# VectorE forms products of whole groups, ScalarE sums them and takes one silu a group, and four rows of a tile change engines

## The reference

```
h = einsum('btc,pc->btp', silu(einsum('btd,cd->btc', x, W_up) + b_up), W_down) + b_down
... scores of two sets of 64 keys for 8 heads, top 8 of each, top 8 of their 64 sums -> sc, indices
de = down_embed[indices]                  # 64 rows of 256 for every token
ue = up_embed[indices]                    # 64 rows of 512 for every token
z = einsum('btd,bthkd->bthk', h, de)      # 64 dot products with h
z = silu(z * softmax(sc))
out = einsum('bthk,bthkd->btd', z, ue)    # weighted sum of 64 rows
x = layernorm(x + out)
```

## Time and profile before

| | us |
|---|---|
| runs: median (lowest to highest) of 3 | 3196.2 (3188.67 to 3196.66) |
| span of the profiled execution, first to last instruction | 3168.2 |
| runs above that span | 20.5 to 28.5 |
| TensorE busy | 2818.4 |
| VectorE busy | 2783.2 |
| ScalarE busy | 2105.8 |
| GpSimd busy | 2098.0 |

### The profile page before, as it was taken

The page is one execution under the profiler, slowest core; times in us unless marked ns, Lnnn a source line. Parts: engine busy times, 40 slices in busy tenths (PEclk is TensorE's granted clock), DMA queues, the critical chain, the costliest instruction groups (busy, mean ns, idle before and its releaser), DMA issues.

```text
span 3168.2 us, 39919 instructions
## 1 busy us (share of the span) xinstructions
PE 2818.4 (89%) x9216; PEld 1501.1 (47%) x9216; DVE 2783.2 (88%) x10160; ACT 2105.8 (66%) x6641; POOL 2098.0 (66%) x2056
## 2 busy tenths in 40 slices
PE   7998999999899999999999999899899999998963
PEld 4444455545454545444445444444445454444431
DVE  3488999999989899999999899898999999898987
ACT  4476766767776667776666677666676666677642
POOL 0067666677667677666667767667766666766676
PEclk9999999999999999999999999999999999999986
DMA  8078888888888788888888888888888888888888
GB/s 289 16 265 277 276 270 269 274 283 289 275 270 267 261 282 293 279 281 269 269 275 300 263 277 280 265 268 291 270 278 275 271 275 290 282 279 275 269 296 280
DMA packets 189837, 856.45 MB, mean 270 GB/s; under 512 B 36192, under 2 KB 39392, under 8 KB 189088
## 3 DMA queue, kind: packets, MB, share of 16 engines
q0 software_dynamic: 163840, 805.44, 76.5%
q1 hardware_dynamic: 19104, 34.87, 3.2%
q10 hardware_dynamic: 6656, 13.60, 1.2%
HBM read 845.38 MB, written 8.39 MB: 269 GB/s over the span
## 4 chain that ended last, share of the span: by engine, by line
PE 57%; POOL 11%; DVE 10%; DMA 10%; ACT 6%; issue 6%; SPq 0%; DVEq 0%; ACTq 0%; POOLq 0%
PE bank L465 14%; POOL ring L279 11%; DMA ring<-embed,idx 10%; PE bank L508 8%; PE bank L362 7%; PE bank L481 6%; PE bank L342 5%; DVE bank L1166 4%; PE bank L496 4%; PE bank L444 3%; PE bank L371 3%; ACT xc L691 3%; DVE ring L1152 2%; PE bank L472 2%; ACT raw L688 1%
## 5 line engine op out<-in xcount | busy, mean ns | idle before, releaser
L279 POOL DMA_INDIRECT ring<-embed,idx x2048 | 2096.7, 1024 | 1057.9 <-issue 544.3
L1166 DVE SCALAR_TENSOR_TENSOR bank<-ring,coef,bank 128x512 f32<-128x512 f32 x1312 | 990.8, 755 | 7.4 <-issue 0.2
L1152 DVE SCALAR_TENSOR_TENSOR ring<-ring,hcur 128x256 f32<-128x256 f32 x2048 | 827.1, 423 | 185.7 <-DMA ring<-embed,idx 182.6
L508 PE MATMUL bank<-ring,diag_c 128*128 128x512 f32 x1344 | 668.8, 628 | 119.6 <-ACT diag_c L666 103.9
L657 ACT ACTIVATE coef<-prob,zp 128x1 f32<-128x1 f32 x2048 | 459.1, 293 | 456.1 <-DVE ring L1152 454.9
L465 PE MATMUL bank<-w_up,zs 128*128 128x512 f32 x1024 | 490.4, 630 | 69.2 <-ACT zs L779 65.8
L508 PEld LDWEIGHTS bank<-ring,diag_c 128*128 128x128 f32 x1344 | 246.6, 199 | 385.8 <-issue 224.9
L465 PEld LDWEIGHTS bank<-w_up,zs 128*128 128x128 f32 x1024 | 200.7, 201 | 329.7 <-issue 238.6
L997 DVE SCALAR_TENSOR_TENSOR xc<-raw,taps,xc 128x128 f32<-128x128 f32 x960 | 266.0, 351 | 53.8 <-ACT xc L691 53.8
L342 PE MATMUL bank<-w_in,ut 128*128 128x512 f32 (+1 forms) x768 | 285.1, 524 | 4.4 <-ACT seg L679 4.3
L666 ACT ACTIVATE diag_c<-cst,coef 128x128 f32<-128x128 f32 x672 | 234.8, 394 | 49.4 <-PE bank L508 38.9
(11 more groups left out here) (147 smaller groups left out, 3685.1 us busy)
## 6 DMA issues: line engine op xcount, KB each, us to landing
ring<-embed,idx POOLq DMA_INDIRECT x2048, 4.6
ring<-uT SPq DMA_DIRECT2D x4, 2048.0 KB, 14.3
ut<-uT SPq DMA_DIRECT2D x32, 256.0 KB, 6.5
zs<-u SPq DMA_DIRECT2D x32, 256.0 KB, 5.7
out<-acc SPq DMA_DIRECT2D x32, 256.0 KB, 4.7
w_up<-W_upT ACTq DMA_DIRECT2D x1, 4096.0 KB, 12.7
w_in<-W_in ACTq DMA_DIRECT2D x1, 2560.0 KB, 17.0
w_in<-W_in ACTq DMA_DIRECT2D x1, 2048.0 KB, 21.5
```

The costliest lines, as they stand in the source:

```text
L279: pool.indirect_dma_start(out=ring[:, k % RING, :], out_offset=None, in_=embed, in_offset=bass.IndirectOffsetOnAxis(ap=idx[:, half, k:k + ...
L508: m = pe.matmul(bank[SUM][:, :], diag_c[:, (len(PE_ROWS) * t + n) % DIAGS, :], ring[:, k % RING, DP:ROW], start=(n == 0), stop=(n == len(P ...
L1152: m = dve.scalar_tensor_tensor(out=ring[:, k % RING, 0:DP], in0=ring[:, k % RING, 0:DP], scalar=1.0, in1=hcur[:, :], op0=ALU.mult, op1=ALU ...
L1166: dve.scalar_tensor_tensor(out=total if n == len(DVE_ROWS) - 1 else running[:, :], in0=ring[:, k % RING, DP:ROW], scalar=coef[:, k:k + 1], ...
```

## The change

Ten groups (3, 5, 7, 8, 9, 10, 11, 13, 16, 19; `SUMMED`), 35 picks of a tile, are handled in another way. VectorE waits for all rows of such a group, multiplies all their 256 numbers by h in one tensor_tensor (`products`), in place in `ring`, and goes on to the weighs of group g-2, which now stand behind the product without dots between them. ScalarE copies each row's products over themselves with the pick's `prob` as scale and sums them into `zp`, waits for its own last sum (`zp_ok`), and takes one silu over the whole group. Groups 1, 13, 16 and 19 turn one P into D: TensorE has 17 rows a tile instead of 21, VectorE weighs 47 instead of 43.

```diff
-GROUPS = ("DD", "PPPD", "DD", "DDD", "PPD", "DDD", "DD", "DDD", "PDDD", "DDD", "DDD", "DDDD", "PDD", "PPPD", "PP", "PDD", "PPPP", "D", "DDD", "PPPD", "D", "PDD")
+GROUPS = ("DD", "PPDD", "DD", "DDD", "PPD", "DDD", "DD", "DDD", "PDDD", "DDD", "DDD", "DDDD", "PDD", "PPDD", "PP", "PDD", "PPPD", "D", "DDD", "PPDD", "D", "PDD")
+SUMMED = (3, 5, 7, 8, 9, 10, 11, 13, 16, 19)
...
                 act.wait_ge(dot_ok, NGRP * t + g + 1)
-                for k in range(FIRST[g], FIRST[g + 1]):
-                    m = act.activation(coef[:, k:k + 1], prob_v[:, k:k + 1], ACT.Silu, scale=zp[:, k:k + 1])
+                if g in SUMMED:
+                    for k in range(FIRST[g], FIRST[g + 1]):
+                        m = act.activation(ring[:, k % RING, 0:DP], ring[:, k % RING, 0:DP], ACT.Copy,
+                                           scale=prob_v[:, k:k + 1], accum_out=zp[:, k:k + 1])
+                    m.then_inc(zp_ok, 1)
+                    act.wait_ge(zp_ok, len(SUMMED) * t + SUMMED.index(g) + 1)
+                    m = act.activation(coef[:, FIRST[g]:FIRST[g + 1]], zp[:, FIRST[g]:FIRST[g + 1]], ACT.Silu)
+                else:
+                    for k in range(FIRST[g], FIRST[g + 1]):
+                        m = act.activation(coef[:, k:k + 1], prob_v[:, k:k + 1], ACT.Silu, scale=zp[:, k:k + 1])
                 m.then_inc(coef_ok, 1)
...
+            def products(t, g):
+
+                lo, hi = FIRST[g], FIRST[g + 1]
+                for k in range(lo, hi):
+                    dve.wait_ge(row_in[k % RING], 16 * (uses(k) * t + k // RING + 1))
+                of = ring[:, lo % RING:lo % RING + hi - lo, 0:DP]
+                dve.tensor_tensor(of, of, hcur[:, :].unsqueeze(1).to_broadcast([P, hi - lo, DP]), ALU.mult).then_inc(dot_ok, 1)
...
+                if g in SUMMED:
+                    products(t, g)
                 for n in range(max(len(mine), len(late))):
-                    if n < len(mine):
+                    if n < len(mine) and g not in SUMMED:
                         dot(t, mine[n], n == len(mine) - 1)
```

More of the change, by code:

```diff
@@ L69 @@
 assert FIRST[NGRP] == PICKS and FIRST[NEW] < RING
+SUMMED = (3, 5, 7, 8, 9, 10, 11, 13, 16, 19)
+assert all(FIRST[g] % RING < (FIRST[g + 1] - 1) % RING for g in SUMMED)
 def signal_of(k):
@@ L211, in build @@
                              "dcy_ok", "st_ok", "rr_ok", "bn_ok", "x1_ok", "h_ok"))
+        zp_ok = sem("zp_ok")
         top1_ok, found_ok, pair_ok, top2_ok, pick_ok, ixy_ok, idx_ok, soft_ok, dot_ok, row_used, sum_ok, r2_ok, o_ok = (
```

## The result

The changed kernel takes **3457.0 us** (3445.9 to 3481.3, four runs) against 3194.4 for the kernel before (3188.7 to 3196.7): a ratio of 1.0843, interval 1.0800 to 1.0887. It is 8.4% slower. The forecast was 3270, range 3190 to 3330: the sign was right, the size was 76 us where 263 were measured.

The account below looks back on a forecast made before the run. No single engine bounds it: VectorE's dots, ScalarE in order, then TensorE open the tile; VectorE and gathers carry its end. 1.85 + 0.6 + 0 = +2.45 us by 30 tiles, plus 2, gives 3272, so 3270; range 3190 to 3330.

Parts of the forecast that it names:

- Reading of before: Whole tile: shares name no owner; VectorE's dots wait 182.6 us for rows, and VectorE and gathers carry search to next groups.
- The prices: Cost per instruction: ScalarE product row 0.48 us (0.40 to 0.61), VectorE product 0.87 us for three rows, 1.14 for four.
- One of the forecast's signs: ScalarE in the changed profile: little left of its waits for VectorE's dots, which were 455 us in the run.
- (a) Tile start: Residual to w_up: VectorE's step 3 adds 0.65 us, ScalarE's uncovered group 5 adds 1.2, so x1T comes 1.85 later.
- (b) The clock: w_up matmuls: a longer TensorE gap makes the slow 1.2 GHz sort the rule, +0.6 us a tile (0 to +2.2).
- (c) Up to the keys' scores: TensorE carries the tile there and ScalarE's longer groups are covered: nothing, or +0.4 us if a product row costs 0.61.
- (d) From the search on: Search to next residual: VectorE's added work, landings and gathers 0.86 us earlier together give 0 (-0.86 to +0.6) a tile.
- The faster rival: TensorE's relief at groups 13 and 16 starts gathers sooner, -1.72 us a tile, 3145 us; chance 0.14.
- The gathers as the bound: Rival: two products in the search-to-residual stretch each hold a gather, +2.3 us a tile more, 3341 us; chance 0.07.
- The 20 to 28 us: Outside the profiled span: runs lie 20 to 28 us above it, and that offset was taken to stay.

Follow-up runs that it names:

- e4: Kernel before with the new table of groups alone: four rows a tile moved from TensorE to VectorE; 3122.6 us, ratio 0.9788.
- e5: Changed kernel with the weighs ahead of the products (as e1) and group 5 not summed; 3226.2 us, ratio 1.0130.
- e2: Kernel before with the changed VectorE order alone: in the ten groups, wait for all rows, all dots, then weighs; 3323.7 us, ratio 1.0424.
- e3: Kernel before with ScalarE's part alone: it sums 35 rows, one silu a group; VectorE's order and dots kept; 3281.6 us, ratio 1.0265.
- e1: Changed kernel with the weighs of group g-2 issued before the product on VectorE; 3257.4 us, ratio 1.0214.
- e6: Changed kernel with group 13 taken out of the summed groups; 3314.7 us, ratio 1.0409.
- e12: Kernel before with group 13's one row alone moved from TensorE to VectorE; 3111.2 us, ratio 0.9767.
- e7: Changed kernel with dots in place of the product, still behind the whole-group wait and ahead of the weighs; 3471.0 us, ratio 1.0877.
- e9: Kernel before with the new table of groups and 14 ring slots, slot fixed as k mod 14; 3233.5 us, ratio 1.0146.
- e11: Kernel before with the new table of groups and 14 ring slots counted on from tile to tile; 3109.0 us, ratio 0.9760.

## Why the prediction was right or wrong, step by step

**Reading of before.** That the shares name no owner held (e4 is faster with a fuller VectorE). Wrong was the reading of VectorE's 182.6 us of waits for rows as a slack that landings decide. Those waits were one end of a loop (row, dot, coefficient, weigh, slot, gather, row) that closes through 13 slots, and they were short because a weigh stood between two dots and kept GpSimd going at 1.25 us a row. The forecast asked what the product costs. It didn't ask what is queued behind the product's wait, which the order had shown.

**The prices** held. A product row on ScalarE was put at 0.48 us:

```profile
1640.53 0.53 ACT L661 ACTIVATE ring<-ring,prob 128x256 f32<-128x256 f32 x1
1640.93 0.22 ACT L661 ACTIVATION_READ_ACCUMULATOR ring<-ring,prob 128x1 f32 x1
1641.03 0.52 ACT L661 ACTIVATE ring<-ring,prob 128x256 f32<-128x256 f32 x1
...
1642.27 0.58 ACT L699 ACTIVATE raw<-bank 128x512 f32<-128x512 f32 x1
```

These are rows of group 5: 0.40 to the read and 0.10 for it, and 1.74 us from 1640.53 to what follows the group, where 1.76 were forecast. ScalarE's busy time rose by 363 us; 390 were forecast. VectorE's products take 1.15 us of four rows (1674.17 to 1675.32), forecast 1.14. One of the forecast's signs failed: little was to be left of ScalarE's waits for VectorE, and there are 302.9 us for dots and 166.0 for products, 469 against 455 before.

**(a) Tile start**, +1.85: right in kind, somewhat large. The stage up to w_up grew by 1.42 us and the gap reached 3.34, not 4:

```profile
1644.79 8.83 PE L468 MATMUL bank<-w_up,zs 128*128 128x512 f32 x16 [3.34 <-ACT zs L790]
```

e5 shows that group 5 is the cause, as the forecast said.

**(b) The clock**, +0.6: right in size, though the share that it was worked out from is misread. In the trace of the kernel before there are 32 rows of sixteen w_up matmuls, 19 of the long sort and 13 of the short (the forecast has 13 long of 19), so the same sum is 13/32 x 1.70 = 0.69. In the changed kernel 29 of the 32 take 8.74 us or more, and the stage from w_up to h grew by 0.63 us. The window (us, then busy us of each engine, granted clock, DMA share, GB/s) at that stage's start, behind the 3.34 us gap:

```profile
1644.00:1648.00 4.00, 3.21 (x4) 1.46 (x5) 3.79 (x14) 4.00 (x14) 3.08 (x4) 0.61 0.84 234
```

0.61 is mostly the lower level of 1.2 GHz, as in the earlier trace rows. Over the span the granted clock went from 0.956 to 0.911, with the engines waiting more; e2 has 0.954 and is 135 us slower than before, so the order costs this without the clock. What the lower clock costs the changed kernel's other stages no run separates; TensorE is busy 2865.1 us there with the 8960 matmuls that take 2706.1 in e4, and some of that may be the clock's.

**(c) Up to the keys' scores, "nothing"**: this is the step that failed. The stage between h and MAX8 grew by 3.83 us. The forecast looked for ScalarE's longer groups there and rightly found them covered (e3: 4.89 us, no change). What it left out is VectorE's wait for group 13 as a whole with group 11's weighs behind it; e1, e2 and e6 each turn that term on or off; in e1, which takes it away, 200 us go.

**(d) From the search on, 0 (-0.86 to +0.6)**: wrong as a sum, and two opposite terms stood in it. The stage ahead of the scan grew by 1.57 us and that up to the residual by 1.09. ScalarE's sums alone cost 1.7 ahead of the scan (e3). In the changed kernel the order costs there too (e1 gives 1.85 back), though alone it makes the stage 1.96 shorter (e2). TensorE's shorter group 13 gives: alone, the stage is 2.3 us shorter (e12). The forecast let the gathers behind group 14 start 0.86 earlier. In the changed kernel they start later: the first of them (pick 56) waits 7.4 us in the mean for TensorE, 2.4 before, and pick 59's starts 1.25 us behind the wide product instead of 0.02.

**The faster rival** (TensorE's relief starts the gathers sooner) was right in its mechanism, for one part of the change: e4 and e12 have it. It priced each row at the row's own 0.86 us on TensorE. Group 13's measured 73 us, 2.3 a tile.

**The gathers as the bound**, by VectorE's products holding them: the hold is there, but it isn't what made up the loss. In the changed kernel 132 gathers are issued while a product runs, and the 68 of them behind products of four rows take 1.63 us in the mean (the rows are in the last section). GpSimd's busy time is 34 us over that of the earlier trace rows, and 92 us over that of e7, which has dots in the products' place and takes the same time. The Trainium skill, "SBUF — State Buffer", section "Who interferes with whom", has a VectorE instruction with two SBUF inputs contend with a GpSimd instruction that reads SBUF; the 2.37 us of the earlier trace rows agree with that, and so does e12, where those gathers come ahead of the wide product. The products of 1.15 us agree too.

**What lies around the span.** The 20 to 28 us that the forecast carried along isn't there: the changed kernel's profiled execution took 3462.6 us with a span of 3460.8. The profiled execution of the kernel before was itself some 20 us quicker than the listed runs, so its tile in the table is about 0.7 us short of a median one. It made no difference to the sum, which added a change to the median.

**What stays open.** The parts alone give -66 (e4), +93 (e3) and +135 us (e2), together +161 before rounding, and the whole is +263. e1 tells where the missing 102 come in: it has ScalarE's sums and the moved rows without the harmful order and costs 68 us, where the two alone make 26, so 42 us arise there (e1's order, weighs first, isn't quite that of the kernel before). On top of e1 the order costs 200 us, against 135 alone; the kernel before is 5 us apart between the two sets of runs.

The table tells at which place. Between h and the search the parts add up: 4.14 (e2), -0.12 (e3) and -0.07 (e4) make 3.95, and the whole has 3.83. Ahead of the scan they don't: -1.96, +1.70 and -1.22 make -1.48, and the whole has +1.57. In e2 and in e4 the gather of pick 59 starts 1.88 and 1.72 us ahead of the wide product, so both are spared the same held gather; in the whole it starts 1.25 us behind the product's start, and neither saving is there. Pick 59's gather is late there because pick 56's gather waits for group 14's rows on TensorE. In the tile shown above, ScalarE waits for VectorE's dots of group 15, and TensorE, ahead of those rows, for line 738, which is behind them on ScalarE:

```profile
1687.18 0.67 ACT L668 ACTIVATE coef<-prob,zp 128x1 f32<-128x1 f32 x3 [3.34 <-DVE ring L1163]
...
1690.34 1.06 PE L382 MATMUL bank<-cst,xc 128*128 128x128 f32 x8 [3.07 <-ACT seg L738]
```

This wait of TensorE is 2.88 us a tile in the changed kernel, 0.78 in e2, 0.01 in e1, and there is none before, in e3 or in e4. So VectorE's late step 13 reaches the gathers a second time there. Why it costs more in the whole than in e2 isn't shown, nor where e1's 42 us come from: no run has the order and ScalarE's sums without the moved rows.

## What to carry to other kernels

Before putting one wait for many in place of many waits for one, look at what stands behind it in that engine's order: if the work that frees buffers for the awaited transfers is there, the wait feeds itself. Put such work ahead of the wait, which here was worth 200 us for a change of two lines. A buffer ring that is counted in slots should count on over the loop's turns (e9 and e11 differ in this alone, 3233.5 and 3109.0 us). Whether a stop of the engine that issues the transfers matters is read from its own rows: where it ran without a break before, there is nothing to make the stop up with.

## What the runs showed of the hardware

The read of the accumulator on ScalarE, 0.22 us long in the rows, adds 0.10 us between the starts, less than half of its length. One tensor_tensor over four rows takes 1.15 us where four dots with their sums take 1.36; over a whole run the exchange didn't show (3457 against 3471 us, intervals overlapping).

A gather that is issued while one of VectorE's products runs, 0.2 us or more behind its start, is held until the product ends. A product of four rows of the changed kernel, and the gather issued 0.29 us behind its start:

```profile
1648.61 1.22 DVE L1174 TENSOR_TENSOR ring<-ring,hcur 128x1024 f32<-128x1024 f32 x1 [0.68 <-DMA ring<-embed,idx]
...
1648.90 1.75 POOL L282 DMA_INDIRECT ring<-embed,idx  x1 [0.30 <-issue]
```

The product ends at 1649.83 and the gather at 1650.65, 0.82 us later. Of the 55 gathers issued so into products of four rows, 53 end 0.82 us behind the product's end and two 0.92 and 0.93; the 21 issued so into line 1014 in the kernel before all end 0.81 or 0.82 us behind its end. Fifteen gathers of the two kernels that were issued 0.2 to 0.95 us ahead of the 2048-wide product took 0.96 us in the mean, as if it weren't there.
